# A mixture-of-experts layer and a gated recurrence in one kernel: recurrent weights turned on VectorE from small-run loads, biases loaded from ScalarE's queue, tile work one scan step later, three rows of gate inputs copied directly

## What is computed

```
h      = gelu(einsum('nc,ech->enh', xf, W1e)); y = einsum('enh,ehc->enc', h, W2e)
routed = einsum('ne,enc->nc', combine, y)          # two experts of eight per token
shared = silu(xf @ w1) * (xf @ w3) @ w2
x1 = x + (shared + routed) / 3
Xz, Xr, Xh = x1 @ Wxz.T + bxz, x1 @ Wxr.T + bxr, x1 @ Wxh.T + bxh
for t in range(512):                               # H starts as cond_1024, 8 x 256
    Z = sigmoid(Xz[t] + H @ Whz.T + bhz)
    R = sigmoid(Xr[t] + H @ Whr.T + bhr)
    C = tanh(Xh[t] + R * H @ Whh.T + bhh)
    H = Z * H + (1 - Z) * C
    Y[t] = H @ Whq.T + bhq
out = x1 + Y
```

## Time and profile before

| | |
|---|---|
| median of 3 runs | 1277.98 us |
| the profiled execution | 1277.44 us |
| span of its instructions | 1275.5 us |
| TensorE, matmul | 1249.8 us, 98% |
| TensorE, weight load | 890.8 us, 70% |
| VectorE | 997.2 us, 78% |
| ScalarE | 803.3 us, 63% |
| GpSimd | 7.4 us, 1% |
| DMA, mean | 40 GB/s |

### The profile page before, as it was taken

The page is one execution under the profiler, slowest core; times in us unless marked ns, Lnnn a source line. Parts: engine busy times, 40 slices in busy tenths (PEclk is TensorE's granted clock), DMA queues, the critical chain, the costliest instruction groups (busy, mean ns, idle before and its releaser), DMA issues.

```text
span 1275.5 us, 84499 instructions
## 1 busy us (share of the span) xinstructions
PE 1249.8 (98%) x35704; PEld 890.8 (70%) x35704; DVE 997.2 (78%) x6111; ACT 803.3 (63%) x4402; POOL 7.4 (1%) x25
## 2 busy tenths in 40 slices
PE   9999999999999999999999999999999999999887
PEld 8877677766677776667776667776667776666554
DVE  6678888788787888878888787887877787877765
ACT  4366666666666666666666666666666666666554
POOL 1000000000000000000000000000000000000000
PEclk9999999999999999999999999999999999999999
DMA  8211011111101111011111101111011111001110
GB/s 273 57 36 43 24 38 30 42 41 34 36 24 39 38 37 45 24 37 27 44 39 35 38 21 41 35 39 45 27 33 27 44 39 33 23 21 27 33 32 11
DMA packets 76186, 51.34 MB, mean 40 GB/s; under 512 B 40609, under 2 KB 73761, under 8 KB 75809
## 3 DMA queue, kind: packets, MB, share of 16 engines
q1 hardware_dynamic: 75128, 45.29, 13.7%
q10 hardware_dynamic: 680, 0.66, 0.2%
HBM read 29.13 MB, written 16.78 MB: 36 GB/s over the span
## 4 chain that ended last, share of the span: by engine, by line
PE 93%; DVE 3%; ACT 2%; issue 1%; DMA 1%; SPq 0%
PE dn_ps L1083 27%; PE up_ps L1111 26%; PE zc_bank L1247 21%; PE r_bank L1247 14%; PE aux L1083 2%; DVE terms L1006 2%; PE dn_ps L1119 1%; ACT t_h L713 1%; PE misc L1083 1%; DVE hist L1009 1%; DMA x_all<-in_L_cond_W1e 1%; DVE t_rT L982 1%; ACT t_r L693 0%; DVE rhT L985 0%; SPq L411 0%
## 5 line engine op out<-in xcount | busy, mean ns | idle before, releaser
L982 DVE STREAM_TRANSPOSE t_rT<-t_r 128x32 f32<-128x32 f32 x1024 | 156.2, 191 | 171.1 <-ACT t_r L693 163.6
L693 ACT ACTIVATE t_r<-r_bank 128x32 f32<-128x32 f32 x1024 | 146.1, 195 | 210.2 <-PE r_bank L1247 200.2
L713 ACT ACTIVATE t_h<-zc_bank 128x32 f32<-128x32 f32 x1024 | 145.9, 195 | 207.7 <-PE zc_bank L1247 207.7
L1083 PE MATMUL dn_ps<-we_sb,x_all 128*32 128x256 f32 (+1 forms) x5144 | 274.5, 329 | 0.0
L1247 PEld LDWEIGHTS zc_bank<-whT,rhT 128*8 128x8 f32 x8192 | 118.1, 87 | 177.5 <-DVE rhT L985 176.9
L1247 PE MATMUL r_bank<-whT,hist 128*8 128x64 f32 x8192 | 210.1, 220 | 16.0 <-DVE hist L1009 13.4
L1247 PE MATMUL zc_bank<-whT,rhT 128*8 128x64 f32 x8192 | 211.0, 220 | 2.8 <-DVE rhT L985 0.3
L1247 PE MATMUL zc_bank<-whT,hist 128*8 128x64 f32 x8192 | 208.9, 219 | 0.8 <-issue 0.8
L1006 DVE STREAM_TRANSPOSE terms<-t_h 128x32 f32<-128x32 f32 x1024 | 156.5, 192 | 38.2 <-ACT t_h L713 19.7
L1247 PEld LDWEIGHTS r_bank<-whT,hist 128*8 128x8 f32 x8192 | 117.6, 88 | 94.6 <-DVE hist L1009 72.5
L1083 PEld LDWEIGHTS dn_ps<-we_sb,x_all 128*32 128x32 f32 x5144 | 137.9, 110 | 31.9 <-issue 1.0
(11 more groups left out here) (132 smaller groups left out, 1691.4 us busy)
## 6 DMA issues: line engine op xcount, KB each, us to landing
gate_inputs_by_group<-gru_raw SPq DMA_DIRECT2D x64, 192.0 KB, 2.0
gru_raw<-gate_inputs_by_group SPq DMA_DIRECT2D x256, 48.0 KB
xT_all<-in_x SPq DMA_DIRECT2D x448, 8.0 KB
x_all<-in_x SPq DMA_DIRECT2D x31, 128.0 KB
out<-gru_raw SPq DMA_DIRECT2D x31, 128.0 KB
x_all<-in_L_cond_W1e SPq DMA_DIRECT2D x4, 512.0 KB, 7.6
we_sb<-in_L_cond_W2e SPq DMA_DIRECT2D x4, 512.0 KB, 8.6
xT_all<-in_L_cond_w SPq DMA_DIRECT2D x2, 256.0 KB, 5.3
```

Of the source, the lines that this page charges most:

```text
L693: act.activation(t_r[:, i, :], r_ps[:, i * Q:(i + 1) * Q], ACT.Tanh, scale=0.5).then_inc(tr_ready, 1)
L713: act.activation(t_h[:, i, :], c_ps[:, i * Q:(i + 1) * Q], ACT.Tanh, scale=-1.0).then_inc(th_ready, 1)
L982: dve.transpose(t_rT[:, i, :], t_r[:, i, :]).then_inc(trT_done, 1)
L1083: done = pe.matmul(ps[Q * j:Q * (j + 1), col:col + cols], lhsT[:, Q * j:Q * (j + 1)], rhs, start=first, stop=last, tile_position=(0, Q * j ...
```

## The change

The seven recurrent weights are no longer transposed by TensorE. SyncE loads them in pieces whose contiguous runs are 32 floats (the three input weights, `load_wx`, 12 DMAs) or 64 floats (the four recurrent ones, `load_blocks`, 16 DMAs), laid out so that VectorE's 32 x 32 transposition of a 128 x 256 tile puts them right: two instructions per weight, fourteen in all (`turn_wx`, `turn_wh`). The factor 0.5 of one weight is put in by one ScalarE instruction (`whh_halved`). The seven bias loads move from SyncE's queue to ScalarE's (`load_biases`). `FIRST_STEP` goes from 6 to 7, so all tile work lies one scan step later, the prologue does three slots of down products instead of four, and 34 ups instead of 36. In the steady tables, half of one projection moves to gap 2 of slot 2 (`PROJ2`), the output product is spread over slots 2 and 5 (`OUT2`, `OUT1`), and bias additions come one slot earlier, at the same step. The first three rows of tile 0's gate inputs are copied from `xproj` to `xs` inside SBUF (`step_rows`, six DMAs per half), the rest still goes over DRAM, and the two late tile loads come behind all of it on SyncE's queue.

```diff
-        FIRST_STEP = 6
+        FIRST_STEP = 7
-        PROJ1 = {2: (-2, 0, 0), 3: (-2, 0, 1), 4: (-2, 1, 0), 5: (-2, 1, 1), 18: (-1, 0, 0), 19: (-1, 0, 1), 20: (-1, 1, 0), 21: (-1, 1, 1)}
+        PROJ1 = {2: (-2, 0, 0), 3: (-2, 1, 0), 4: (-2, 1, 1), 18: (-1, 0, 0), 19: (-1, 1, 0), 20: (-1, 1, 1)}
+        PROJ2 = {2: (-2, 0, 1), 18: (-1, 0, 1)}
+        OUT1 = {5: -4, 21: -3}
+        OUT2_PARTS, OUT1_PARTS = [(0, 1, 2)], [(0, 0, 1), (1, 0, 2)]
...
-        BIAS2 = {3: (0, -2), 5: (1, -2), 19: (0, -1), 21: (1, -1)}
-        FINISH2 = {2: -4, 18: -3}
+        BIAS2 = {2: (0, -2), 4: (1, -2), 18: (0, -1), 20: (1, -1)}
+        FINISH2 = {5: -4, 21: -3}
...
-        FIRST_UPS = 36
+        FIRST_UPS = 34
         UP_FIRST, begin = {}, FIRST_UPS
-        for r in [r for r in range(FIRST_R, SPAN - 1) if r not in LAST_DOWN2]:
-            end = begin + (3 if r in X1_2 else 5 if r in LOGITS2 or r in (12, 13, 14, 25, 29) else 6)
+        for r in [r for r in range(FIRST_R, SPAN - 1) if r not in LAST_DOWN2 and r not in PROJ2]:
+            end = begin + (3 if r in X1_2 else 5 if r in LOGITS2_FIRST or r in (12, 13, 14) else 6)
...
+            def load_blocks(blocks, w, loaded):
+
+                by_row = w.rearrange("(n r) c -> r n c", r=Q)
+                for j in range(NG):
+                    sp.dma_start(blocks[Q * j:Q * (j + 1), :, :], by_row[:, :, GW * j:GW * (j + 1)]).then_inc(loaded, 16)
+
+            def load_wx(g):
+
+                by_row = gru_wx[g].rearrange("(n r) (k c) -> r k n c", r=Q, k=KC)
+                for j in range(NG):
+                    sp.dma_start(wx_blocks[g][Q * j:Q * (j + 1), :, :, :], by_row[:, :, :, Q * j:Q * (j + 1)]).then_inc(ld_wx[g], 16)
...
+            def step_rows(s, q):
+
+                for j in range(q * NG // PIECES, (q + 1) * NG // PIECES):
+                    sp.dma_start(xs[Q * j:Q * j + B, s, :], xproj[s::TS, j, :]).then_inc(xs_step[s], 16)
...
+            act.wait_ge(wh_turned, GATES * NI)
+            act.activation(whT[:, 2, :, :], whT[:, 2, :, :], ACT.Copy, scale=0.5).then_inc(whh_halved, 1)
             consume_up(1, 1)
-            act.wait_ge(xs_first, 16 * NG)
+            act.wait_ge(xs_step[0], 16 * NG)
             seed_r(0, 0)
             seed_zc(0, 0)
-            consume_up(1, 2)
...
+            def turn_wh(g):
+
+                dve.wait_ge(ld_wh[g], 16 * NG)
+                for i in range(NI):
+                    dst = whT[:, g, i, :] if g < GATES else wqT[:, i, :]
+                    dve.transpose(dst.rearrange("p (n r) -> p n r", r=Q), wh_blocks[g][:, :, Q * i:Q * (i + 1)]).then_inc(wh_turned, 1)
...
-            gate_biases()
+            turn_wx(2)
             accumulate(0, NE)
             accumulate(1, 0)
-            for q in range(PIECES):
-                add_bias(0, q)
+            gate_biases()
+            add_bias(0, 0)
+            turn_wh(0)
+            add_bias(0, 1)
+            turn_wh(1)
+            turn_wh(2)
             shared_silu(1, 0)
             shared_hidden(1, 0)
+            turn_wh(3)
             shared_silu(1, 1)
```

More of the change, by code:

```diff
@@ L151, in moe_then_gru @@
         ld_h0 = sem("ld_h0")
-        ld_gru_x = sem("ld_gru_x")
-        ld_gru_h = sem("ld_gru_h")
+        ld_wx = [sem(f"ld_wx{g}") for g in range(GATES)]
+        ld_wh = [sem(f"ld_wh{g}") for g in range(GATES + 1)]
+        wx_turned = sem("wx_turned")
+        wh_turned = sem("wh_turned")
+        whh_halved = sem("whh_halved")
         ld_bias = sem("ld_bias")
@@ L190, in moe_then_gru @@
         xs_second = sem("xs_second")
+        xs_step = [sem(f"xs_step{s}") for s in range(AHEAD)]
         bits_set = sem("bits_set")
@@ L243, in w13_cols @@
             return slice(half * HS // 2, (half + 1) * HS // 2)
-        def in_round(e):
-            sizes = [len(HEAD_TR)] + [len(r) for r in ROUND_TR]
-            return range(sum(sizes[:e + 1]), sum(sizes[:e + 2]))
         def evacuate(m):
-            kind, i = GROUPS[m]
+            kind, i = HEAD_TR[m]
             src = tr_ps[m % 2]
@@ L323, in moe_then_gru @@
         for r, tile in OUT2.items():
-            GAP2[r] = in_slots("out", 0, tile, NI)
+            GAP2[r] = [("out", 0, tile, *part) for part in OUT2_PARTS]
         for r, tile in LAST_DOWN2.items():
@@ L562, in take @@
                 act.activation(dst, src, ACT.Copy, scale=s).then_inc(tr_act, 1)
-            def take_round(e):
-                for m in in_round(e):
-                    if m % 2 == 0:
-                        take(m)
             def score_tanh(i, tiles):
@@ L649, in _, with load_biases @@
                 act.dma_start(w3_raw[:, :, cols], w3[:, cols].rearrange("(k p) h -> p k h", p=P)).then_inc(ld_w13[half][1], 16)
+            def load_biases(gate):
+                for dst, src in ((bias_x, gate_bx[gate]), (bias_h, gate_bh[gate])):
+                    act.dma_start(dst[:, gate, :], src.rearrange("(a c) -> a c", a=1).to_broadcast([P, C])).then_inc(ld_bias, 16)
             act.wait_ge(zeros_ready, 1)
@@ L1187, in tile_logits, with output @@
                     done.then_inc(logits_done, 1)
-            def output(t, i):
-                if i == 0:
+            def output(t, i, begin, end):
+                opens = (i, begin, end) == OUT2_PARTS[0]
+                if opens:
+                    if t == 0:
+                        pe.wait_ge(wh_turned, NI * (GATES + 1))
                     pe.wait_ge(yst_ready, t + 1)
@@ L1221, in fill_up @@
                         down(*piece)
-                    if scan and not downs:
+                    outs = r in OUT1 and 0 <= 2 * p + OUT1[r] < NT - 1
+                    if outs:
+                        for part in OUT1_PARTS:
+                            output(2 * p + OUT1[r], *part)
+                    if scan and not downs and not outs and not (r in OUT1 and 2 * p + OUT1[r] < 0):
                         keep_busy()
@@ L1232, in fill_rest @@
                     up(pair, m, tiles)
+                if r in PROJ2 and 0 <= 2 * p + PROJ2[r][0] < NT:
+                    tile, q, k = PROJ2[r]
+                    project(2 * p + tile, q, k)
                 for kind, g, tile, part, begin, end in GAP2[r]:
@@ L1237, in fill_rest @@
                     elif kind == "out" and 0 <= t < NT - 1:
-                        output(t, part)
+                        output(t, part, begin, end)
                 if scan and r in UP_GAP2 and not ups:
                     keep_busy()
-                if r in LOGITS2 and EARLY <= 2 * p + 2 + LOGITS2[r][0] < NT:
-                    tile_logits(2 * p + 2 + LOGITS2[r][0], LOGITS2[r][1])
+                logits_at = first_or(p, LOGITS2_FIRST, LOGITS2)
+                if r in logits_at and EARLY <= 2 * p + 2 + logits_at[r][0] < NT:
+                    tile_logits(2 * p + 2 + logits_at[r][0], logits_at[r][1])
             def gate_product(ps, gate, lhsT, k):
@@ L1298, in _ @@
             early_logits()
[L1299 removed]
             for e in range(NE):
                 unit(0, NSH + e)
[L1302 to L1308 removed]
+                whole_down(0, e)
             for k in range(NSH // 2):
```

148 lines of the change are left out of this document (63 added, 85 removed).

## The result

The changed kernel takes 1282.42 us (median of 22 runs, 1278.63 to 1285.05), the one before 1278.45 us in the same session (22 runs, 1276.40 to 1281.59): a ratio of 1.0024, 95% interval [1.0017, 1.0032]. In a second session it was 1.0015 [1.0005, 1.0026]. By these ratios it is slower by 2 to 3 us (the medians of the first session are 4.0 apart). The prediction said 1276.6, between 1274.5 and 1279.0.

The account below looks back on a forecast made before the run. It took the chain through the state to bound each scan step, so only an earlier start wins: -2.0 + 0.1 + 0.55 = -1.35 us, from 1277.98 to 1276.6 us; own range 1275.7 to 1277.6, over all 1274.5 to 1279.0.

Parts of the forecast that it names:

- slower in every tile: Rival, scan: the moved half bias addition starts 0.1 us late in each of 32 tiles, +3.2 us, 1279.8; chance 0.05.
- The 0.5 us wait for the accumulation: Prologue: TensorE waits 0.5 us for VectorE near 25.1, so 2.3 of the 2.8 us of removed groups is kept.
- VectorE's chain from the first bias addition to the last accumulation: Prologue: from 40.81 to 47.2 with eight transpositions at 0.38 us; TensorE waits 1.2 us for its end.
- my 2.0: Start of the scan: first gate product at 48.8 instead of 50.81, 2.0 us earlier.
- no waits: Rival, prologue: TensorE keeps all 3.7 us, less 0.1 and 0.55, giving 3.05 us gained, 1274.9 us; chance 0.24.
- ScalarE's queue: Rival, prologue: bias loads issued by ScalarE at twice the price start the scan 1 us later, 1277.7; chance 0.13.
- The first six: Prologue on VectorE: six of fourteen weight transpositions take the place of four copies and idle time, costed at nothing.
- my own case: Whole kernel: scan starts 2.0 us earlier, net -1.35 us, 1276.6 us, range 1275.7 to 1277.6; chance 0.50.
- the rival of the late small runs: SyncE's weight loads: at 1.2 us per issue the third recurrent weight comes late, scan at 53, 1280.8 us; chance 0.08.
- The direct rows are hidden behind VectorE either way: Seeds at the scan's start: rows copied inside SBUF land at 46 to 48, before 48.8, costed at nothing.
- Slot 15: First pair of tiles, scan step 6: a matmul waits for ScalarE's gelu, 0.55 us lost once.
- My sign for the scan: Scan: steps of 2.377 us elsewhere, so last step minus first stays unchanged within 1 us.

Follow-up runs that it names:

- wx_long_runs: Changed kernel with the twelve input-weight loads in 2 KB runs instead of 128 bytes, so weights are permuted; ratio to the kernel before 0.9995 [0.9982, 1.0007].
- wx_256_more: Changed kernel with input weights in 256-byte runs, slot 15's up one slot later, direct rows for steps 0 and 1 only; 1277.57 us, 0.9985 of the kernel before.
- row0_first: Changed kernel with SyncE issuing both halves of row 0, then of rows 1 and 2, then the two stores; ratio to the kernel before 1.0026 [1.0016, 1.0036].

## Why the prediction was wrong

**What held.** The chain through the state sets the step (2.375 against 2.377), and steady steps did not grow in either half: rival "slower in every tile" is out. The 0.5 us wait for the accumulation came as 0.40. The turns cost 0.34 us each where I took 0.38 (four in a row fill 44.09 to 45.43), so VectorE's chain from the first bias addition to the last accumulation was 5.3 us to its start where the working had 5.9, and TensorE waited 0.35 instead of 1.2. With weight and rows in time (`wx_long_runs`, `wx_256_more`) the prologue was 3.0 us shorter, between my 2.0 and the 3.7 of "no waits". ScalarE's queue was no bound: its bias loads took 0.33 to 0.64 us each to issue. The working has one slip, on which nothing rests: 511 steps exceed 511 x 2.373 by 5.0 us, not 5.1.

**The step that failed.** "The first six fall where VectorE now does four copies and has idle time, and I cost them at nothing." VectorE had the time. What was short was the weight: the third lands at 38.6, 6 us behind its last issue, and the bias addition comes 1.5 us later than forecast. That is where "no waits" and my own case both end. I had the piece that decides it, in the rival of the late small runs, and put 0.08 on it because nothing tied the issue time to bytes. The rows could not show it: the cost is in the transfer, at a full DMA share. A 128-byte-run load that was not held took 0.63 us to issue, inside my 0.52 to 0.64 (0.42 in runs of 2 KB). I also hung the rival on the third recurrent weight; it was the third input weight that was late, while the recurrent ones landed 2.0 to 2.6 us after their issue (median of each weight's four).

The Trainium skill (DMA: Bandwidth & Descriptors, Specifications) gives 512 bytes as the least transfer that reaches line rate. By that rule the case was the likeliest, and the trace agrees with it: 127 GB/s in 128-byte runs at the share that moved 346, and 151 GB/s in 256-byte runs. At 256 bytes, still below its bound, the start was no longer held by the weight.

The change has one more part that the working passes over: before, SyncE issues the three input weights' loads from 11.09 to 13.64, among the experts' weights, and now from 20.94 on, behind them all. At that place long runs are in time and 128-byte runs are not. What was not tried: the 128-byte-run loads at the earlier place; the late tile loads ahead of the rows; and the bias loads back on SyncE's queue. So it is not shown whether the short runs could be kept at no loss.

**"The direct rows are hidden behind VectorE either way."** They were not: 43.48 instead of 41.4 for the first, 0.60 us each where a row read from DRAM takes 0.37 (2.97 / 8), and the second half of row 0 behind five other issues. The seed came at 50.11, not at 46 to 48. Undoing one part of the order did not bring the gain back, since two bounds of nearly the same time stood one behind the other: the seed's (`row0_first` removes it) and the weight's (`wx_long_runs` removes it, and ends the weight loads ahead of the rows at 37.60 instead of 43.35).

**The scan.** Slot 15 was right in kind and sized 0.55 for 0.76. The wait for row 1 (0.35 to 0.37) was not in the sum, and neither was step 11 (0.28 to 1.20 in the changed kernel, up to 2.86 where the start was earlier). The diff moves `load_late(EARLY)` from 30.2 to behind the rows; its 17 issues, some 11 us, were in my working only as a price for a small load, not as work moved past a queue. My sign for the scan, last step minus first unchanged within 1 us, failed: 1220.9 in the first profile against 1217.6.

So 2.0 us earlier became 0.7 later on the mean of four, and 0.65 us of stalls became 1.6. My 1277.44 was also the luckiest of four executions, 1.9 us under their mean in the late scan. The medians of the sessions suffer less: 1278.45 to 1279.59 for the kernel before, where I started from 1277.98.

## What to carry to other kernels

When a load is cut into shorter runs, ask for the transfer and not for the issue: hold the GB/s at full DMA share against the bytes that must be there, and look at who stands behind the first consumer in program order. When issues are added to a queue, list everything that is now behind them, down to loads that are needed 30 us later. A gain ahead of several bounds of similar time appears only when all are moved: here longer runs gave 2 to 3 us, and edits of two kinds that had given nothing by themselves (slot 15, the order of the rows) gave almost 2 more behind them. And before two single profiles are compared, measure from a point that the change does not touch: here the start wandered by up to 1.3 us ahead of it.

## What was not expected of the hardware

- Executions of the same kernel differ by up to 1.3 to 3.9 us in scattered steps of 0.03 to 1.4 us late in the scan (3.4 to 7.3 over in four profiles of one program). A few of them are tied to the program: three steps (37, 85, 211) were over by 0.14 to 0.18 in all four profiles of before, seven by 0.09 to 0.28 in all four of the changed one. The others move. What they are was not tried.
- A copy from SBUF to SBUF of one row (6 KB) took 0.56 to 0.68 us to issue, against 0.30 for most of those from DRAM, of up to eight times the bytes (48 KB).
- One wait of 1.96 us on TensorE was followed by some 3 us at the lower clock; waits of 1.32, 1.46 and even 2.03 us were not.
